# Layer-norm statistics taken over two tiles in one instruction, and the step that combined them left out

## What is computed

```python
def _layernorm(x, axis=-1, eps=1e-05):
    m = jnp.mean(x, axis=axis, keepdims=True)
    v = jnp.var(x, axis=axis, keepdims=True)
    return (x - m) / jnp.sqrt(v + eps)
```

## Time and profile before

| what | value |
|---|---|
| median of 3 runs | 5075.74 us (5071.69 to 5084.2) |
| span of the profiled execution | 5060.6 us |
| what lies around the span | 15.1 us, if the profiled execution took the median |
| instructions | 85,606 |

### The profile page before, as it was taken

One profiled execution on the slowest core, in us unless ns is written; L12 is line 12 of the kernel. 1 busy time (PEld: TensorE's weight loads), 2 busy tenths in 40 slices (PEclk: granted clock), 3 DMA queues, 4 the chain that ended last, 5 costly groups with the idle time before them and its releaser, 6 DMA issues. The chain is left out here.

```text
span 5060.6 us, 85606 instructions
## 1 busy us (share of the span) xinstructions
PE 3780.0 (75%) x21997; PEld 2986.0 (59%) x22311; DVE 4095.2 (81%) x20404; ACT 3645.4 (72%) x9165; POOL 3833.6 (76%) x3164
## 2 busy tenths in 40 slices
PE   6537777877677778888868888888788786766664
PEld 4326666665556666776745666666566565645443
DVE  7659999988999997887778788888699897756564
ACT  0048898987777777777768788888678686766564
POOL 7777887875777776888766877776588886777777
PEclk9868999988888899999979899999899898877777
DMA  8977777776666666766659889888466554333332
GB/s 253 320 216 211 195 199 201 199 194 151 161 159 158 152 142 147 163 153 154 144 143 257 240 242 256 233 243 207 123 142 153 131 132 101 103 93 95 96 95 70
DMA packets 837877, 864.14 MB, mean 171 GB/s; under 512 B 89656, under 2 KB 621174, under 8 KB 837382
## 3 DMA queue, kind: packets, MB, share of 16 engines
q1 hardware_dynamic: 512124, 566.02, 34.7%
q0 software_dynamic: 219520, 232.07, 26.8%
q10 hardware_dynamic: 105738, 60.56, 4.3%
HBM read 339.16 MB, written 523.51 MB: 170 GB/s over the span
## 5 line engine op out<-in xcount | busy, mean ns | idle before, releaser
L1238 POOL DMA_INDIRECT node<-sage_comb,leadd x392 | 635.2, 1620 | 181.3 <-DMA node<-sage_comb,leadd 99.8
L474 PE MATMUL dense_p<-ident,dense_h 128*128 128x128 f32 x1956 | 335.8, 299 | 348.4 <-ACT dense_h L468 338.7
L468 ACT ACTIVATE dense_h<-dense_x,dense_n_shift,dense_n_rstd 128x128 f32<-128x128 f32 x1304 | 534.1, 486 | 74.6 <-DVE dense_n_shift L457 73.5
L474 PEld LDWEIGHTS dense_p<-ident,dense_h 128*128 128x128 f32 x1956 | 236.5, 151 | 445.4 <-ACT dense_h L468 425.5
L1238 POOL DMA_INDIRECT sums<-mlp_same,leadh x196 | 320.5, 1635 | 129.0 <-issue 60.2
L484 PE MATMUL dense_p<-wT,dense_hT 128*128 128x128 f32 x2608 | 372.8, 290 | 51.3 <-ACT dense_hT L1073 21.7
L1238 POOL DMA_INDIRECT node<-gcn_comb,leads x196 | 322.8, 1647 | 99.2 <-issue 41.0
L484 PEld LDWEIGHTS dense_p<-wT,dense_hT 128*128 128x128 f32 x2608 | 374.6, 207 | 20.6 <-issue 6.2
L1238 POOL DMA_INDIRECT sums<-mean_comb,leads x196 | 323.5, 1651 | 82.9 <-DMA sums<-mean_comb,leads 43.0
L1073 ACT ACTIVATE dense_hT<-dense_p 128x512 f32<-128x512 f32 x489 | 285.5, 588 | 48.3 <-PE dense_p L474 47.2
L465 ACT ACTIVATE dense_n_std<-dense_n_mean_var,eps 128x4 f32<-128x4 f32 x652 | 188.9, 294 | 154.1 <-DVE dense_n_mean_var L451 150.0
(11 more groups left out here) (322 smaller groups left out, 13951.4 us busy)
## 6 DMA issues: line engine op xcount, KB each, us to landing
node<-b SPq DMA_DIRECT2D x392, 256.0 KB
sums<-zero_row SPq DMA_DIRECT2D x392, 256.0 KB
node<-zero_row ACTq DMA_DIRECT2D x49, 1152.0 KB
dense_x<-in_x SPq DMA_DIRECT2D x163, 256.0 KB
out<-dense_y SPq DMA_DIRECT2D x163, 256.0 KB
x_src<-xs SPq DMA_DIRECT2D x49, 256.0 KB, 5.9
y_dst<-gcn_y SPq DMA_DIRECT2D x49, 256.0 KB, 3.5
sage_xs<-x_src SPq DMA_DIRECT2D x49, 256.0 KB, 3.1
```

Source lines behind the costliest of these rows:

```text
L468: tiles(lambda t: nc.scalar.activation(out[:, t, :], x[:, t, :], func, bias=b.sh[:, t:t + 1], scale=b.rs[:, t:t + 1])).then_inc(done, 1)
L474: return tiles(lambda t: nc.tensor.transpose(ps[:, t * P:(t + 1) * P], x[:, t, :], ident))
L1238: pool.indirect_dma_start(table, bass.IndirectOffsetOnAxis(ap=leads[:, i * G + c, t:t + 1], axis=0), e.comb[c][:, t, :], None, element_off ...
```

## The change

`stats` becomes two instructions instead of four. Each reads two tiles interleaved (feature 0 of tile t, feature 0 of tile t+1, feature 1 of tile t, ...), so that the even elements are one tile and the odd ones the other, and the six numbers that are written are count, mean and summed squared deviation of either tile. Nothing is left to combine: `mean_var` goes, `shift` reads the mean where it lies, and `std` divides the summed squares by 128 in its scale. In SBUF two elements that are read one after the other lie 512 bytes apart.

```diff
-LN = (("stats", VECTOR, 790), ("mean_var", VECTOR, 310), ("std", SCALAR, 205), ("rstd", VECTOR, 95),
-      ("shift", VECTOR, 80), ("norm", SCALAR, 1545))
+LN = (("stats", VECTOR, 680), ("std", SCALAR, 205), ("rstd", VECTOR, 95), ("shift", VECTOR, 80), ("norm", SCALAR, 1545))
...
-        self.st = sb(name + "_stats", [P, T, 6], F32)
-        self.mv = sb(name + "_mean_var", [P, T, 2], F32)
+        self.st = sb(name + "_stats", [P, T, 3], F32)
...
+def pair_stats(nc, st, x):
+    for t in range(0, T, 2):
+        last = nc.vector.bn_stats(st[:, t:t + 2, :].rearrange("p t k -> p (t k)"), x[:, t:t + 2, :].rearrange("p t f -> p f t"))
+    return last
...
     if name == pre + "stats":
         dve.wait_ge(done, at.before(i, name))
-        tiles(lambda t: nc.vector.bn_stats(b.st[:, t, :], x[:, t, :])).then_inc(done, 1)
-    if name == pre + "mean_var":
-        dve.wait_ge(done, at.before(i, name))
-        tiles(lambda t: nc.vector.bn_aggr(b.mv[:, t, :], b.st[:, t, :])).then_inc(done, 1)
+        pair_stats(nc, b.st, x).then_inc(done, 1)
...
-        nc.vector.scalar_tensor_tensor(out=b.sh[:, :], in0=b.mv[:, :, 0], scalar=-1.0, in1=b.rs[:, :],
+        nc.vector.scalar_tensor_tensor(out=b.sh[:, :], in0=b.st[:, :, 1], scalar=-1.0, in1=b.rs[:, :],
...
-        nc.scalar.activation(b.sd[:, :], b.mv[:, :, 1], ACT.Sqrt, bias=eps).then_inc(done, 1)
+        nc.scalar.activation(b.sd[:, :], b.st[:, :, 2], ACT.Sqrt, bias=eps, scale=1.0 / D).then_inc(done, 1)
...
-        FILL = ("weigh", "x_mean_var", "x_norm", "y", "lead", "match", "combine", "keep")
+        FILL = ("weigh", "x_stats", "x_norm", "y", "lead", "match", "combine", "keep")
```

## The result

The changed kernel takes 5091.99 us (median of six, 5089.15 to 5104.87) against 5075.39 us (six, 5071.69 to 5084.2): ratio 1.0038 with a 95% interval of 1.0026 to 1.005, slower by 0.4%. The profiled execution took 5091.56 us for a span of 5089.8.

A forecast was written before the change was run, and what follows sets the result against it. POOL, issuing back to back with 0.30 us gaps, was taken as the bound (4777 us, 94% of the span). Savings of 6 + 4 + 2 + 2 + 4 = 18 us gave 5058 us, range 5030 to 5100.

The forecast's parts named there:

- 1.07 to 0.70 us a norm, 508 us of DVE: Statistics and aggregation on DVE: 0.37 us saved for each of 1,372 norms, 508 us of DVE's 4,095.
- The interleaved read at 0 ns: New statistics instructions: reading elements 512 bytes apart adds 0 ns an element, at most 1.25.
- Rival D: New statistics instructions: the strided read is slow, saving gone at 0.72 ns an element; 5111 to 5180 us; chance 0.12.
- The sum of 18 us: Whole kernel: shortened waits for compute and barriers together save 18 us, bounds 0 and about 60.
- sage1's first add: Start of sage1: POOL's 10.63 us wait falls to about 4, 6 us saved.
- mlp's second round: Second round of gathers in mlp: POOL's 9.68 us wait falls to about 6, 4 us saved.
- mlp's end: Near mlp's end: POOL's 12.81 us wait gets 2 us shorter.
- The barriers behind gcn: Five barriers between stages, waits of 3.71 to 12.47 us: 4 us saved over all, between 0 and 35.
- The three short waits of sage1: POOL's short waits for L1533 in sage1, such as 1.28 us: 2 of 3 us saved together.
- mean's 5.07: A POOL wait of 5.07 us in mean, ending on PE in a chain without a norm before it: 0 saved.
- rival C: All queues: the re-made order costs POOL what the relief gives, or more; twelve more 3 us waits, 5094 us; chance 0.16.
- What lies around the span: Time outside the profiled span: 15.1 us, added to the forecast span of 5042.6 to give 5057.7.

The follow-up runs named there:

- e6: e1 with one statistics instruction per norm instead of two, tiles 2 and 3 normed with the statistics of tiles 0 and 1: 5039.88 us, ratio 0.9936.
- e4: e1 with the two statistics instructions of each norm run twice, first into a spare buffer, in the old order: 5253.32 us.
- e5: e1 with each statistics instruction reading its 256 elements in a row instead of two tiles interleaved: 5053.39 us.
- e1: The new statistics instructions issued in the exact order of the kernel before, the aggregation's place left empty: 5055.25 us, ratio to before 0.9953.
- e7: e1 with all due times of the second stream of edges in mean 300 us later: 5087.44 us, ratio 1.0036.
- e3: The changed kernel with all due times of the second stream of edges in mean 300 us earlier: 5067.47 us, ratio 0.9979.
- e11: The kernel before, no instruction changed, the planner told 810 instead of 790 for a norm's statistics: 5203.77 us, ratio 1.0252.
- e10: The kernel before, no instruction changed, the planner told 770 instead of 790 for a norm's statistics: 5204.17 us, ratio 1.0246.
- e9: The changed kernel in its own re-made order, the two statistics instructions of each norm run twice, first into a spare buffer: 5595.57 us.

## Why the prediction was wrong

- *POOL bounds the kernel*: right. POOL's busy time and its 0.30 us gaps are unchanged, gcn stays over 900 us, final does not shorten, and e6 gets 15 us for 423 of DVE. In e4, with DVE busy for 4,479 us, POOL alone no longer sets the time: 198 us more of it for 19 more of POOL's busy time.
- *1.07 to 0.70 us a norm, 508 us of DVE*: right; 0.67 us a norm, DVE's busy time down by 478.
- *The interleaved read at 0 ns*: right, 0.02 (e5). Rival D needed 0.72. The Trainium skill's rule that supported D ("Advanced Engine Details and Errata", section Memory Cachelines: accesses that each touch another line pay) shows no more than 5 of 420 ns in this instruction's time; the measurement decides. (The prediction's 195 us for D are 4% of the time behind the setup and 5% of DVE's; nothing else hangs on it.)
- *The sum of 18 us*: near in size for the instructions, 21 us (e1), but by luck, since its places were wrong. sage1's first add was to wait 6 us less than 10.63 and still waits 11.02 us in e1, and 10.81 and 12.03 in e5 and e7, although DVE is busy there in e1 for 50.8 of 61.5 us and no longer for 57 of 63: that chain was not late for want of DVE. mlp's second round gave 1.2, not 4. mlp's end gave more, 12.81 to 7.56. The barriers behind gcn gave more too: all five together were 41.7 us in before and are 34.8 in e1, 34.4 in e5 and 29.3 in e7, where I took 4 off. The three short waits of sage1 shrank to one of 0.84, and mean's 5.07 stayed, as forecast.
- *Two signs came true for another reason.* In the kernel after, sage1's first add waits 0.30 us (I had named about 4) and mlp's second round 5.61 (about 6), in POOL's timeline of after:

```profile
1317.65 2.02 POOL L1228 DMA_INDIRECT node<-sage_comb,leadd  x1 [0.30 <-DMA sage_agg<-node,gsrc]
...
2682.49 1.24 POOL L615 DMA_INDIRECT mlp_a<-node,gsrc  x1 [5.61 <-DVE mlp_v L1874]
```

With the same instructions in the old order these waits are 11.02 and 8.44 us, so most of what was gained here is the new order's and not the relief's.
- **The step that failed** is that the re-made order costs nothing in the sum: it stood apart as rival C with a chance of 0.16. With the same instructions the new order costs 5092 - 5055 = 37 us, and C's 5094 us is what was measured. That the number fits is luck: C had twelve more 3-us waits in mid-stage, and what cost the time was in the main one stream left alone at mean's end; mean has ten POOL waits of 2.4 us and more in either kernel, and three of them grew to 41 us. By stage, after minus e1 is 36.6 us in mean and 12.5 in sage1; sage2 is 5.7 shorter. sage1's loss comes back in other executions: it lasts 694 and 698 us in the new order (after, e3) and 681 to 683 in the old one (e1, e5, e7). There POOL has 17 waits of 2.4 us and more in after and in e3, against 11 to 14 in e1, e5 and e7, so a little of C's own form may be in it. My argument against C, that POOL's own lengths and due times were unchanged, does not hold: the order comes from all engines' lengths together.
- *What lies around the span*, 15.1 us, was wrong too: in every later run it is 1.7 to 2.2. The execution whose rows I read was thus one of about 5062 us, 13 under the median.

That the order costs the time, and not the instructions, is shown by e1; that in mean it does so by one stream, by e3 and e7. Why the same due times leave that stream behind under the shorter length, and which change of order costs sage1 its 12 us, was not tried.

## What to carry to other kernels

Where a static plan sets the order, a change of one length is two changes: change the instruction and keep the order first (a node that issues nothing does it), measure, and only then let the plan move. Read the written order for a chain that ends alone before a barrier; it can be read before anything runs. It does not tell all: in e11 no stream ends alone, and mean is the longest of the table. And relief of an engine that isn't the bound was worth little here below the knee (0.04 to 0.05 us a us) and much above it (0.46), so one slope does not carry over.

## What was not expected

Twenty ns of a planned length, with no instruction changed, moved this kernel from 5076 to 5204 us (e10, e11). And two orders of the same instructions bear a longer DVE at 0.23 and 0.57 us a us (e4, e9): how much slack an order has for an engine's steps does not show in the time at which it runs undisturbed, 5055 and 5092.
